# Sorted experts with two segments interleaved in DRAM and a copy moved to ScalarE; inverse roots of the second attention by Newton steps on VectorE

## What is computed

```
logits = x @ gate_w.T;  scores = sigmoid(logits)
topk_idx = top_k(scores + expert_bias, 4);  w = scores[topk_idx] / sum
y = sum over k of w_k * ( silu(x @ wg_e.T) * (x @ wu_e.T) ) @ wd_e.T   +   shared expert
```

```
_ln(t) = (t - mean) * rsqrt(var + 1e-6) * w + b      over the 16 numbers of a head
```

## Time and profile before

| what | value |
|---|---|
| median of 3 runs | 1144.42 us |
| time of the profiled execution | 1144.54 us |
| span of its profile | 1143.2 us |
| mean granted clock of TensorE | 0.928 |
| busy: PE, VectorE, ScalarE, GpSimd | 953.8, 739.7, 509.8, 344.9 us |

### The profile page before, as it was taken

The page is one execution under the profiler, slowest core; times in us unless marked ns, Lnnn a source line. Parts: engine busy times, 40 slices in busy tenths (PEclk is TensorE's granted clock), DMA queues, the critical chain, the costliest instruction groups (busy, mean ns, idle before and its releaser), DMA issues.

```text
span 1143.2 us, 14811 instructions
## 1 busy us (share of the span) xinstructions
PE 953.8 (83%) x4834; PEld 678.8 (59%) x4834; DVE 739.7 (65%) x1884; ACT 509.8 (45%) x1268; POOL 344.9 (30%) x289
## 2 busy tenths in 40 slices
PE   5677679999999999999986977977778888976556
PEld 2222234668989998888864755754445555544445
DVE  5899994245666667677754536657567855567653
ACT  3574461136666665566621322334356542132331
POOL 3477791131111112144106405446551100010110
PEclk9787899999999999999998999997899999989677
DMA  8400001010111172123003435323000003211100
GB/s 320 190 1 0 1 0 47 0 42 29 43 42 42 42 271 76 42 74 98 1 10 111 129 106 160 120 81 93 1 1 1 1 2 133 70 42 35 74 19 19
DMA packets 36037, 73.44 MB, mean 64 GB/s; under 512 B 4077, under 2 KB 21239, under 8 KB 35321
## 3 DMA queue, kind: packets, MB, share of 16 engines
q1 hardware_dynamic: 32024, 62.76, 16.4%
q0 software_dynamic: 3072, 8.39, 2.3%
q10 hardware_dynamic: 864, 1.34, 0.3%
HBM read 50.72 MB, written 21.76 MB: 63 GB/s over the span
## 4 chain that ended last, share of the span: by engine, by line
PE 55%; DVE 13%; POOL 6%; DMA 4%; issue 4%; ACT 2%; SPq 1%; another core or an unknown queue 1%; POOLq 0%; DVEq 0%; ACTq 0%
PE psum L2041 5%; PE psum L946 5%; PE psum L1138 4%; PE psum L1149 4%; PE psum L807 4%; PE psum L1118 3%; PE psum L949 3%; POOL arena L2392 3%; PE psum L1657 3%; DMA arena<-tokens 2%; PE psum L1129 2%; PE psum L818 2%; PE psum L970 2%; PE psum L2060 2%; DVE arena L2331 2%
## 5 line engine op out<-in xcount | busy, mean ns | idle before, releaser
L1028 POOL TENSOR_TENSOR arena<-arena,mhalf 128x8 f32<-128x8 f32 x32 | 53.7, 1679 | 258.4 <-DVE arena L1013 258.4
L1250 DVE SCALAR_TENSOR_TENSOR X<-psum,arena,X 128x256 f32<-128x256 f32 x128 | 55.9, 478 | 67.8 <-PE psum L1149 65.6
L418 POOL TENSOR_TENSOR arena<-arena 128x512 f32<-128x512 f32 x64 | 83.5, 1331 | 7.5 <-DVE arena L735 4.2
L1657 PE MATMUL psum<-arena 128*128 x248 | 69.1, 403 | 9.6 <-issue 8.6
L735 DVE TENSOR_TENSOR_SCAN arena<-psum,arena 128x512 f32<-128x512 f32 x64 | 74.7, 1207 | 3.3 <-ACT psum L610 1.8
L1192 ACT ACTIVATE arena<-psum,arena 128x256 f32<-128x256 f32 x128 | 60.0, 477 | 35.0 <-DVE arena L1229 34.8
L481 PE MATMUL psum<-arena,ident 128*128 128x512 f32 x128 | 72.9, 696 | 0.7 <-POOL arena L418 0.5
L2316 ACT ACTIVATE arena<-psum,arena 128x240 f32<-128x240 f32 x128 | 57.4, 465 | 21.4 <-DVE arena L2336 17.4
L1149 PE MATMUL psum<-arena 128*128 128x256 f32 x256 | 65.9, 380 | 1.2 <-DVE X L1250 1.1
L1138 PE MATMUL psum<-arena 128*128 128x256 f32 x256 | 65.8, 380 | 0.0
L1118 PE MATMUL psum<-arena 128*128 128x256 f32 x256 | 65.8, 380 | 0.0
(11 more groups left out here) (343 smaller groups left out, 2341.8 us busy)
## 6 DMA issues: line engine op xcount, KB each, us to landing
arena<-in_w SPq DMA_DIRECT2D x32, 384.0 KB
tokens<-arena SPq DMA_DIRECT2D x2, 4096.0 KB, 22.6
arena<-tokens SPq DMA_DIRECT2D x30, 256.0 KB
results<-arena SPq DMA_DIRECT2D x30, 256.0 KB
arena<-in_moe SPq DMA_DIRECT2D x17, 384.0 KB, 3.1
arena<-in_moe SPq DMA_DIRECT2D x4, 1536.0 KB, 14.2
arena<-in_w SPq DMA_DIRECT2D x2, 1024.0 KB, 5.9
arena<-in_gu SPq DMA_DIRECT2D x1, 1280.0 KB, 6.2
```

What stands on the lines that cost most here:

```text
L418: nc.gpsimd.tensor_tensor(m.HC[:, v, :], m.Hs[:, v, :], m.Cs[:, s % 2, :], ALU.mult).then_inc(*tick("HC", s, c))
L1250: a = nc.vector.scalar_tensor_tensor(k.X[:, t, :], bank[5][:, j * D:(j + 1) * D], m.ri[:, u % 4, j:j + 1], k.X[:, t, :], ALU.mult, ALU.add)
L1657: mm = nc.tensor.matmul(bank[b][:, 0:D], m.xgT[:, n % 2, c, :], m.W[:, bass.ds(place + c * D, D)], start=c == 0, stop=c == DC - 1)
```

## The change

- `sorted_rows_sp` and `sorted_results_sp` use "(p n) d": rows of segments j and 16+j are interleaved in DRAM, and each partition has one piece of 2 KB. The row numbers are worked out for that with one more VectorE instruction for each half (`second`), the scan starts at -1/128 in place of a later subtraction, and the list of experts by segment is interleaved on the host. The results tensor has 32 segments.
- SyncE issues four loads ahead in place of three. The ring stays at three pairs.
- The copy of the turned hidden activations moves from VectorE to ScalarE, behind SiLU.
- The first six steps take one position of neighbouring work, as all others.
- Half 1's gathers have a buffer for each of the 16 (laid over the expert weights), with one semaphore for two gathers; half 0's pieces on VectorE are spread over 12 positions in place of 8.
- The power on GpSimd and the scaling on VectorE, eight each, are replaced by `a2_root_dve`, four times: twelve VectorE instructions on 64 numbers in each partition.
- The constants and positions are new; keys get one more position between bias and products; in the second attention GpSimd runs gathers, keys and queries side by side.

```diff
 def sorted_rows_sp(k, m, h, i):
...
-    k.nc.sync.dma_start(m.Xr[:, first:first + len(two), :],
-                        k.tokens[h][rows:rows + len(two) * P, :].rearrange("(n p) d -> p n d", p=P)).then_inc(
+    k.nc.sync.dma_start(m.Xr[:, first:first + 2, :],
+                        k.tokens[h][i * 2 * P:(i + 1) * 2 * P, :].rearrange("(p n) d -> p n d", n=2)).then_inc(
         *k.s.landed(f"e_xr{ring}", m.tag, two[0]))
...
-    k.nc.sync.dma_start(k.results[h][rows:rows + len(two) * P, :].rearrange("(n p) d -> p n d", p=P),
-                        m.Ys[:, first:first + len(two), :]).then_inc(*k.s.landed(f"e_ys{ring}", m.tag, two[0]))
+    k.nc.sync.dma_start(k.results[h][i * 2 * P:(i + 1) * 2 * P, :].rearrange("(p n) d -> p n d", n=2),
+                        m.Ys[:, first:first + 2, :]).then_inc(*k.s.landed(f"e_ys{ring}", m.tag, two[0]))
...
-    pairs, ahead = len(m.pairs(0)), m.RING // 2
+    pairs, ahead = len(m.pairs(0)), m.RING // 2 + 1
...
-    nc.vector.tensor_scalar(m.rowk[h], m.pos[:, h], -1.0, None, ALU.add).then_inc(*done("rowk"))
+    nc.vector.tensor_scalar(m.second[:, h], m.pos[:, h], 16.0 * P, 32.0 * P - 1.0, ALU.is_ge, ALU.mult).then_inc(*done("second"))
+    after("second")
+    nc.vector.scalar_tensor_tensor(m.rowk[h], m.pos[:, h], 2.0, m.second[:, h], ALU.mult, ALU.subtract).then_inc(*done("rowk"))
...
         step(beside[h])
-        if h == 0 and n < 6:
-            step(beside[h])
...
+    def hidden_turned(n):
+        act.wait_ge(*at("e_ht_ps", tag, n))
+        if n >= 2:
+            act.wait_ge(*at("e_out", tag, n - 2))
+        nc.scalar.copy(m.HT[:, n % 2, :], bank[4][:, 0:P]).then_inc(*tick("e_ht", tag, n))
...
     def step_of(n):
         if n == total:
             last()
         if n + 2 < total:
             turned(n + 2)
         if n + 1 < total:
             silu(n + 1)
+        if 1 <= n <= total:
+            hidden_turned(n - 1)
...
+def combined_landing(m, h, q):
+
+    return (m.Yg[h][:, q, :], f"e_yg1{q // 2}", q | 1) if h else (m.Yg[h][:, q % m.RING, :], f"e_yg0{q % m.RING}", q)
...
-        if q >= ring:
-            pool.wait_ge(*at("x_e", tag, h, q - ring))
+        if not h and q >= m.RING:
+            pool.wait_ge(*at("x_e", tag, h, q - m.RING))
...
-        if q % 2:
+        if q % 2 or (h == 0 and q % 4 == 0):
             yield
...
+def a2_root_dve(k, m, h, q):
...
+    nc.vector.tensor_scalar(v, v, 1.0 / m.HD, 1e-6, ALU.mult, ALU.add).then_inc(*done("v"))
+    after("v")
+    nc.vector.tensor_scalar(y.bitcast(whole), m.va_flat(q).bitcast(whole), -0.5, float(0x5f3759df), ALU.mult,
+                            ALU.add).then_inc(*done("y"))
+    nc.vector.tensor_scalar(b, m.va_flat(q), -0.5, None, ALU.mult).then_inc(*done("b"))
+    after("b")
+    for i in range(3):
+        nc.vector.tensor_tensor(a, y, y, ALU.mult).then_inc(*done(("square", i)))
+        after(("square", i))
+        nc.vector.tensor_tensor(a, a, b, ALU.mult).then_inc(*done(("product", i)))
+        after(("product", i))
+        nc.vector.scalar_tensor_tensor(y, a, 1.5, y, ALU.add, ALU.mult).then_inc(
+            *(done(("root", i)) if i < 2 else tick("a2_root", q, h)))
...
-    nc.gpsimd.tensor_tensor(root, root, k.mhalf[:, 0:2 * m.NH], ALU.pow).then_inc(*tick("a2_rt", q, b))
-    pool.wait_ge(*at("a2_rt", q, b))
...
-KEYS, KEYS_OVER, COMBINED, QUERIES, OVER = 9, 18, 4, 13, 12
+KEYS, COMBINED, QUERIES, OVER = 13, 5, 17, 9
...
-    attention2_pe(k, a2, (both(later(1, attention2_keys_pe(k, a2, 1, at2, 14)),
-                               later(9, attention2_queries_pe(k, a2, 1, at2, OVER))),
+    attention2_pe(k, a2, (both(later(1, attention2_keys_pe(k, a2, 1, at2, OVER)),
+                               later(12, attention2_queries_pe(k, a2, 1, at2, OVER))),
...
-        both(combined_dve(k, m1, 1, "a2"), later(1, attention2_keys_dve(k, a2, 1, at2, 14)),
-             later(9, attention2_queries_dve(k, a2, 1, at2, OVER))),
+        both(later(3, combined_dve(k, m1, 1, "a2")), later(1, attention2_keys_dve(k, a2, 1, at2, OVER)),
+             later(12, attention2_queries_dve(k, a2, 1, at2, OVER))),
...
-        one_by_one(combined_pool(k, m1, 1), attention2_keys_pool(k, a2, 1, 0), attention2_queries_pool(k, a2, 1, OVER)),
+        both(combined_pool(k, m1, 1), later(9, attention2_keys_pool(k, a2, 1, 0)), later(12, attention2_queries_pool(k, a2, 1))),
...
-    sort[:, 0:32] = np.arange(32)
+    sort[:, 0:32] = np.arange(32).reshape(2, 16).T.reshape(-1)
```

More of the change, by code:

```diff
@@ L1314, in __init__ @@
         self.W = k.place(E * 768)
+        k.at = 29952
+        self.Yg = [None, k.place(self.Q, D)]
         k.at = 15488
@@ L1331, in __init__ @@
         self.slot, self.rank, self.mine = k.place(2, HT, E), k.place(2, HT, E), k.place(2, HT, E)
-        self.pos = k.place(2, self.Q)
+        self.pos, self.second = k.place(2, self.Q), k.place(2, self.Q)
         self.offs = [self.whole(k, S, mybir.dt.int32) for _ in range(2)]
@@ L1398, in sorted_rows_sp @@
     k.sp.wait_ge(*k.s.at(f"e_scatter{h}", m.tag, m.Q - 1))
-    ring, first = m.place_in_ring(two[0])
+    ring, first = m.place(two[0], m.RING)
     before = (m.pairs(0) + m.pairs(1))[:h * len(m.pairs(0)) + i][-(m.RING // 2):]
@@ L1411, in sorted_results_sp @@
     k.sp.wait_ge(*k.s.at("e_y", m.tag, two[-1]))
[L1412 to L1415 removed]
+    ring, first = m.place(two[0], m.YS)
+    k.nc.sync.dma_start(k.results[h][i * 2 * P:(i + 1) * 2 * P, :].rearrange("(p n) d -> p n d", n=2),
+                        m.Ys[:, first:first + 2, :]).then_inc(*k.s.landed(f"e_ys{ring}", m.tag, two[0]))
 def sorted_sp(k, m):
[L1419 removed]
+    pairs, ahead = len(m.pairs(0)), m.RING // 2 + 1
     for i in range(ahead):
@@ L1548, in sorted_head_dve @@
     after("segs")
-    nc.vector.tensor_tensor_scan(ends[:, 1, :], m.one, segs, 0.0, ALU.mult, ALU.add).then_inc(*done("ends"))
+    nc.vector.tensor_tensor_scan(ends[:, 1, :], m.one, segs, -1.0 / P, ALU.mult, ALU.add).then_inc(*done("ends"))
     after("ends")
@@ L1636, in turned @@
         b = n % 2
-        ring, place = m.place_in_ring(n)
+        ring, place = m.place(n, m.RING)
         pe.wait_ge(*at(f"e_xr{ring}", tag, n - n % NS % 2))
@@ L2213, in __init__ @@
         self.va = k.place(4, 2 * NH)
+        k.at = 29056 + 128
+        self.root, self.newton = k.place(2, 4 * NH), k.place(2, 4 * NH)
+        k.at = 14976
         self.Kb, self.Qb = k.place(DC, S), k.place(4, DC, S)
@@ L2380, in a2_variance_dve, with done, after @@
     nc.vector.tensor_reduce(v, m.sq[:, 2 * q + b % 2], AX, ALU.add).then_inc(*tick("a2_v_sum", q, b))
-    dve.wait_ge(*at("a2_v_sum", q, b))
-    nc.vector.tensor_scalar(v, v, 1.0 / m.HD, 1e-6, ALU.mult, ALU.add).then_inc(*tick("a2_v_mean", q, b))
+def a2_root_dve(k, m, h, q):
+    nc, dve, at, tick = k.nc, k.dve, k.s.at, k.s.tick
+    def done(i):
+        return tick("a2_newton", q, h, i)
+    def after(i):
+        dve.wait_ge(*at("a2_newton", q, h, i))
+    v = m.va[:, 2 * q:2 * q + 2, :]
+    y, a, b = m.root[:, q], m.newton[:, 0], m.newton[:, 1]
+    whole = mybir.dt.int32
+    for w in (2 * h, 2 * h + 1):
+        dve.wait_ge(*at("a2_v_sum", q, w))
+        if h:
+            dve.wait_ge(*at("a2_N", q, w - 2))
+    nc.vector.tensor_scalar(v, v, 1.0 / m.HD, 1e-6, ALU.mult, ALU.add).then_inc(*done("v"))
[11 more added lines that the diff above has]
+            *(done(("root", i)) if i < 2 else tick("a2_root", q, h)))
+        if i < 2:
+            after(("root", i))
 def a2_normalised_pool(k, m, h, q, b):
@@ L2429, in attention2_keys_pe @@
         yield
-    v2 = pair(3)[0]
+    v2 = pair(4)[0]
     k.bank_ready(v2)
@@ L2435, in attention2_keys_pe @@
     k.free[v2] = [("a2_V2", h)]
-    for _ in range(over - 3):
+    for _ in range(over - 4):
         yield
@@ L2479, in attention2_keys_dve @@
         a2_variance_dve(k, m, h, 0, b)
-    for _ in range(over - 6):
+    yield
+    a2_root_dve(k, m, h, 0)
+    for _ in range(over - 7):
         yield
@@ L2575, in attention2_queries_dve @@
         a2_variance_dve(k, m, h, 1, b)
-    for _ in range(over - 4):
+    yield
+    a2_root_dve(k, m, h, 1)
+    for _ in range(over - 5):
         yield
@@ L2599, in attention2_queries_pool @@
     if h == 0:
-        for _ in range(over - 6):
-            yield
         pool.wait_ge(*at("a2_aff"))
```

84 lines of the change are left out of this document (37 added, 47 removed).

## The result

The changed kernel takes 1138.52 us (median of 6 runs, 1136.50 to 1138.93), the kernel before 1144.16 us beside it (6 runs, 1141.58 to 1145.73). The ratio is 0.9948, 95% interval 0.9934 to 0.9962: 5.6 us less where I forecast 26.5 less. It lies 0.5 us above the top of the range.

What follows compares the result with a forecast made beforehand. TensorE's own order was taken as the path, so gains are its idle and lower-clock time in two stages. Experts -16.5 and attention -10.0 give -26.5 against 1144.5: 1118 us, range 1096 to 1138.

Steps and rivals of the forecast that it cites:

- Gathers: Attention: with 16 buffers GpSimd issues without waiting for VectorE, taking -6 of VectorE's 6.2 us wait, end 0.
- waits move: Rival: TensorE waits for VectorE and roots instead of loads, so only -11.5 us, 1133 us; chance 0.13.
- Loads, -9: Experts: loads issued earlier remove 9 of TensorE's 10.0 us waiting for tokens, ends 0 and -16.0.
- Copy on ScalarE, -3: Experts, 690 to 718: moving the copy off full VectorE cuts TensorE's idle time by 3 us, ends 0 and -5.
- ScalarE becomes the loop: Rival, experts: the copy waits for its transpose by itself, adding 48 us over 62 steps, 1166 us; chance 0.07.
- Bias wait, -3.5: Experts: later keys with a free position behind the bias remove TensorE's 3.5 us wait, end 0.
- ScalarE's unknown wait, -3: Experts: half of ScalarE's 6.0 us wait with unknown releaser goes, -3 us, ends 0 and -6.0.
- Keys' root, +3.3 and +2.5: TensorE's turn one position behind the keys' root waits +3.3 us in the experts, +2.5 in the attention (ends 0, 4.9).
- Newton, 2.8 us for twelve steps: Root on VectorE: twelve dependent small instructions take 2.8 us, replacing two 5.47 us GpSimd powers for each of four groups.
- A block by GpSimd, +1: Attention: one VectorE root instruction is held up while GpSimd works, +1 us, ends 0 and 4.
- The tokens' root, -5.4: Attention: keys' root of half 1 no longer holds up the tokens' root on GpSimd, removing TensorE's 5.4 us wait.
- Clock, -4 in the attention: TensorE's clock rises where idle time goes: -4 us in the attention, -2 in the experts, ends 0 and -12.

Runs made afterwards that it cites:

- r1_ring3: Changed kernel, but half 1's gathers again wait for VectorE's use of the row three back; 1113.37 us on chip 12, 0.9869 of the kernel before.
- c3_after: Changed kernel with nothing edited, on chip 12; 1106.75 us, 0.9796 of the kernel before.
- u3_ahead3: Changed kernel with each load of a pair of segments issued one pair later, three ahead as before; 1118.43 us on chip 8, 0.9900 of the kernel before.
- u2_copy_vector: Changed kernel with the copy of the turned hidden activations back on VectorE; 1136.82 us on chip 11, against 1137.44 for the changed kernel unedited.
- s2_keys_later: Changed kernel with the turn of the normed keys two positions later in both stages; 1105.54 us on chip 4, 0.9795 of the kernel before.

## Why the prediction was wrong

**The step that failed** is "Gathers": "With 16 buffers GpSimd issues without waiting for VectorE ... -6 of the 6.2 us, end 0". The gain itself is real. Without stalls 16 buffers are worth 6.6 us (r1_ring3 against c3_after), and VectorE's wait for gathers is down to 1.9 us in the first measurement. But the slow end of the term was 0, and what came with the unbroken run on the chip of the first measurement is a stall: 19.1 us of ScalarE's and 13.7 us of VectorE's waits on semaphores of TensorE. With it -6 became +10 in the first eleven steps, since the stretch takes 16.1 us more than the same kernel needs on chip 12. That is most of the 18.4 us between the forecast there (-10.0) and what was measured (+8.4).

The warning was in the rows. ScalarE's 6.0 us wait, "released by something that the profile doesn't know", and a TensorE busy for 4.3 of 11 us stood beside a scatter of 16 that GpSimd issued without a pause. I gave the wait to a "crowded place" and booked -3 for its going, and never asked what ran beside it. It is in the changed kernel again, and it would have priced one more unbroken run of 16 at up to the same 11 us. No rival had this mechanism; "waits move" gave a near time, 1133, by other waits.

Step by step, by the chips without stalls unless said:
- **Loads, -9.** Right in mechanism, a little too small: about 12 by u3_ahead3, 11.7 in the time and 12.2 in the stage.
- **Copy on ScalarE, -3.** No gain seen (u2_copy_vector, on a chip with stalls only). It was read from TensorE's idle time in 690 to 718; that stretch holds the run of ten gathers of half 0 (689.7 to 702.2) and its waits on an unknown releaser, 699.9 to 704.6. The rival that ScalarE becomes the loop fell too: 48 us more would have shown. The end's +0.7 holds: 2.6 us of waiting for it in place of 1.93.
- **Bias wait, -3.5.** Right: 0.4 us is left of it.
- **ScalarE's unknown wait, -3.** Wrong: where it occurs it is still there (8.7 us before L2488 at 628.5), and elsewhere it is in neither kernel.
- **Keys' root, +3.3 and +2.5.** As waits 3.8 and 5.2 us in c3_after, the first nearly right, the second above its end of 4.9; the kernel before on chip 4 has 4.2 for such products, queries included. As a price wrong: s2_keys_later takes them away and gains about nothing.
- **Newton, 2.8 us for twelve steps.** 2.86, from 787.47 to the end of the last step at 790.33 (above). VectorE's 4.8 us on the path can't be read by itself: the first eleven steps had 7.9 us less with them in.
- **A block by GpSimd, +1.** It didn't occur. In the changed kernel of the first measurement, of chip 11 and of chip 12 no GpSimd instruction runs beside any of the four roots, and each takes 2.8 to 2.9 us. So the rule that the forecast named has no case here either.
- **The tokens' root, -5.4.** Gone as forecast; TensorE's L258 waits for nothing but 1.8 us of "issue".
- **Clock, -4 in the attention.** Wrong: 0.85 before and after on the chips without stalls, 0.86 and 0.79 with them. In the experts, where I had -2, it is 0.97 and 0.98 without stalls, 0.93 and 0.95 with them.

The sum, -26.5, is close to what the change does where nothing stalls: the profiled spans differ by 25.2 us (1129.7 and 1104.5), the medians on chip 12 by 20.4. The medians are the better measure, since the profiled run of the kernel before was 3.8 us above its chip's median. Part of that closeness is luck: -3 for the copy, -3 for the unknown wait and -4 of clock were not there, and the loads gave 3 more.

What stays open: what delays TensorE's semaphores, and why on chip 11 and in the first measurement, but not on chips 3, 4, 8, 10 and 12. That the unbroken run causes the stall, and that added pauses cure it, was not shown, since all ten runs with them fell on chips without it; that a stall goes with each unbroken run of seven or more is an observation over 16 runs in one program.

## What to carry to other kernels

A wait that the profile can't attribute is to be matched with what runs beside it before it is priced, and a change that makes more of the neighbour (here an unbroken run of indirect transfers on GpSimd) gets the wait's size as its upper end. Buffers that take away a wait that paces an engine need their own bound on the slow side. Whether such a wait is worth keeping depends on the chip: without stalls it cost 6.6 us here, and with them it was not measured. And a difference of half a per cent on one chip says little of another: the same change gave 0.6% on one chip and 2% on another, and an unedited control belongs in every group of runs.

## What the runs showed of the hardware

- Chips differ in this program by 1.3 to 1.5%: the kernel before took 1144.6 us on chip 11 and 1127.2 to 1129.5 on chips 3, 4, 8, 10 and 12. Between the profiles of the first measurement and of chip 4, 12.8 of 13.5 us lie in the experts' stage, where the first has waits on an unknown releaser beside GpSimd's indirect transfers and the second has none. In the changed kernel the gathers of half 1 are issued every 1.26 us on chips of either kind.
- In such a stall ScalarE is held as VectorE is: 7.95 us ahead of L2750, on a semaphore of TensorE whose event is recorded 7.2 us or more after the work. TensorE's 6.9 us ahead of L2458 follow from that copy. The Trainium skill, SBUF — State Buffer, Who interferes with whom, says that TensorE and ScalarE never wait on anyone for SBUF's ports. No run here tests that sentence, but by it this stall is no port conflict of the kind that held VectorE.
